# Graph network kernel: ranking counters laid out stream by stream, and row keys copied one step ahead

## The reference

```
edge_index = stack([src, dst])
h = relu(layernorm(x))
x = x + gcn(h, edge_index)      # sum over edges of h[src] * norm, by dst; layernorm, relu
h = relu(layernorm(x))
x = x + attention(h, edge_attr_128, edge_attr_128_n2, edge_index)
   # k, v: one row per edge; softmax and weighted sum over the edges of each src node, 4 heads
```

## Time and profile before

| | |
|---|---|
| median of 3 runs | 4865.36 us (4861.69 to 4885.93) |
| profiled execution | 4897.3 us, its span 4895.6 us |
| busy in the span | PE 69%, DVE 58%, ACT 50%, POOL 42% |
| POOL indirect scatters (L550) | 1612, 1894.3 us busy |
| ACT sums (L623) | 1616 activations, 883.3 us, and 308.6 us of accumulator reads |
| DVE products (L718) | 404, 380.1 us |
| DVE comparison with the ruler (L707) | 202, 196.5 us |

### The profile page before, as it was taken

How to read it: one execution, slowest core, us unless ns; L and a number is a source line. 1 busy time by engine, 2 the same in 40 slices (tenths; PEclk the granted TensorE clock), 3 DMA queues, 4 the chain that set the end, 5 groups by cost and what they waited for, 6 DMA issues and landing times. The chain is left out here.

```text
span 4895.6 us, 79918 instructions
## 1 busy us (share of the span) xinstructions
PE 3389.2 (69%) x21299; PEld 2441.0 (50%) x21299; DVE 2855.3 (58%) x5810; ACT 2454.4 (50%) x7415; POOL 2047.4 (42%) x1890
## 2 busy tenths in 40 slices
PE   3488767778777774021454567666668998999898
PEld 2266544455554452011333455555556776777665
DVE  6877787888887673530000455555556777777611
ACT  0545598888898784010232334333334665666411
POOL 1677287777777777777001433333331000000000
PEclk7655579999998897555555788888888999999855
DMA  1554144444444545456211566666666666666400
GB/s 59 168 173 163 49 138 162 155 160 160 161 151 157 170 160 183 142 170 208 88 33 53 187 207 222 216 208 214 212 209 196 189 190 203 189 189 190 132 0 26
DMA packets 511558, 764.21 MB, mean 156 GB/s; under 512 B 53848, under 2 KB 377408, under 8 KB 511358
## 3 DMA queue, kind: packets, MB, share of 16 engines
q1 hardware_dynamic: 406798, 522.56, 35.2%
q0 software_dynamic: 78160, 226.14, 12.2%
q10 hardware_dynamic: 26400, 13.21, 0.9%
HBM read 515.95 MB, written 245.75 MB: 156 GB/s over the span
## 5 line engine op out<-in xcount | busy, mean ns | idle before, releaser
L550 POOL DMA_INDIRECT table_s<-ring,place x1612 | 1894.3, 1175 | 1158.0 <-DMA ring<-in_kv 576.0
L623 ACT ACTIVATE row_base<-row_base 128x196 f32<-128x196 f32 x1616 | 883.3, 557 | 200.2 <-DVE row_base L718 189.5
L1346 PE MATMUL bank<-kT,G 128*128 128x384 f32 x1200 | 573.3, 562 | 235.9 <-ACT kT L1393 139.4
L1393 ACT COPY kT<-bank 128x384 f32<-128x384 f32 x600 | 286.5, 477 | 595.3 <-remote 264.6
L1366 PE MATMUL bank<-kv_rows,exT 128*128 128x129 f32 x3600 | 536.1, 288 | 0.0
L943 PE MATMUL bank<-xres 128*128 128x98 bf16 x3136 | 315.3, 236 | 291.4 <-ACT work L662 192.2
L1437 DVE TENSOR_REDUCE gmax<-bank 128x1 f32<-128x384 f32 x600 | 333.2, 555 | 299.2 <-remote 116.7
L962 PE MATMUL bank<-parts,work 128*128 128x384 bf16 x2401 | 501.2, 367 | 0.0
L1366 PEld LDWEIGHTS bank<-kv_rows,exT 128*128 128x128 f32 x3600 | 486.7, 205 | 0.1
L662 ACT CAST work<-bank 128x392 bf16<-128x392 f32 x784 | 373.1, 510 | 165.4 <-PE bank L943 98.3
L1017 DVE SCALAR_TENSOR_TENSOR others<-kv_rows,node_s,iota_h 128x384 bf16<-128x384 f32 x600 | 371.4, 619 | 135.1 <-DMA kv_rows<-table_s 79.2
(11 more groups left out here) (272 smaller groups left out, 4915.5 us busy)
## 6 DMA issues: line engine op xcount, KB each, us to landing
kv_rows<-table_s SPq DMA_DIRECT2D x600, 408.0 KB, 3.1
ring<-in_kv SPq DMA_DIRECT2D x402, 512.0 KB
G<-G_dram SPq DMA_DIRECT2D x600, 64.5 KB, 2.7
table_s<-ring,place POOLq DMA_INDIRECT x1612
G_dram<-gst ACTq DMA_DIRECT2D x50, 258.0 KB
x_dram<-xres SPq DMA_DIRECT2D x1, 3200.0 KB, 15.2
out<-ring SPq DMA_DIRECT2D x1, 3072.0 KB
table_s<-parts SPq DMA_DIRECT2D x6, 136.0 KB, 3.8
```

The costliest lines, as they stand in the source:

```text
L550: pool.indirect_dma_start(out=m["table_s"], out_offset=bass.IndirectOffsetOnAxis(ap=m["place"][0:n, i, k:k + 1], axis=0), in_=m["ring"][0: ...
L623: last = nc.scalar.activation(at, at, ACT.Identity, accum_out=m["place_f"][:, i % 2, h * STREAMS // 2 + k:h * STREAMS // 2 + k + 1])
L1346: pe.matmul(scores[k][:, 0:SGE], m["G"][:, u, 0:P], m["kT"][:, k, :], start=False, stop=True, skip_group_check=True).then_inc(m["scored"], 1)
```

## The change

**Layout.** A slot of the 1568 was tile * 8 + stream and is now stream * 196 + tile. The comparison, the four banks (two streams each now), the base rows, the products and what the sums read all follow. The ruler is stored once (196 elements) instead of eight times; in the comparison the ruler is now repeated over the streams, and the key is repeated along the 196 innermost elements. Before, the ruler was read as it lay, and eight keys side by side were repeated over the tiles. What ACT sums is now 196 elements side by side; they were four elements (16 bytes) apart.

**Halves.** The first half of the products now needs only the first two banks, so PE signals `ranked` twice per step, and `count` adds to two banks after each half of the products instead of to all four after both.

**Keys.** POOL copies the keys of step i + 1 before it issues the DMAs of step i (two copies in step 0). For that the rows of step i - 2 must have been sent, where it was i - 3.

**Shares.** `POOL_STEPS` goes from (132, 156) to (130, 152): two scatter steps leave the scatter block, the nodes block has 22 instead of 24, the last layer 50 instead of 46. The gathers' places are scaled with it: the first three stand behind POOL's step 27 instead of 28.

```
-POOL_STEPS = (132, 156)
+POOL_STEPS = (130, 152)
...
-        last = dve.tensor_copy(m["second_row"][one, :].rearrange("p (t s) -> p t s", s=STREAMS), m["second_base"][one, :, b * tiles:(b + 1) * tiles].rearrange("p s t -> p t s"))
+        last = dve.tensor_copy(m["second_row"][one, :], m["second_base"][one, :, :].rearrange("p s t -> p (s t)")[:, b * LANES_BANK:(b + 1) * LANES_BANK])
...
-            nc.scalar.copy(m["ruler"][:, :, :], column(m["iota_t"][:, :], [P, STILES, STREAMS])).then_inc(m["ruler_ready"], 1)
+            nc.scalar.copy(m["ruler"][:, :], m["iota_t"][:, :]).then_inc(m["ruler_ready"], 1)
...
 def scatter_rows(m, pool, i):
     u, first = i % KRING, STREAMS - columns(i)
-    need(pool, m["rows_sent"][u], sent_before(i))
-    pool.tensor_copy(m["ring"][:, u, first:STREAMS, KEY_AT:KEY_AT + 1], m["sources"][:, i, first:STREAMS].rearrange("p (s a) -> p s a", a=1)).then_inc(m["keys_ready"], 1)
+    for j in ((0, 1) if i == 0 else (i + 1,) if i + 1 < STEPS else ()):
+        v, at = j % KRING, STREAMS - columns(j)
+        need(pool, m["rows_sent"][v], sent_before(j))
+        pool.tensor_copy(m["ring"][:, v, at:STREAMS, KEY_AT:KEY_AT + 1], m["sources"][:, j, at:STREAMS].rearrange("p (s a) -> p s a", a=1)).then_inc(m["keys_ready"], 1)
     pool.wait_ge(m["places_ready"], i + 1)
     pool.wait_ge(m["rows_loaded"][u], 32 * (i // KRING + 1))
     pool.wait_ge(m["keys_ready"], i + 1)
...
-                        at = m["products"][:, h, :, k:k + 1].rearrange("p t a -> p (t a)")
+                        at = m["products"][:, h, k, :]
...
             def hot(i):
                 need(dve, m["counted"], i - 1)
-                dve.tensor_tensor(m["among"][:, i % 2, :].rearrange("p (t s) -> p t s", s=STREAMS), m["ruler"][:, :, :],
-                                  row_of(m["keys_t"][:, i, :], [P, STILES, STREAMS]), ALU.is_equal).then_inc(m["hot_ready"], 1)
+                dve.tensor_tensor(m["among"][:, i % 2, :].rearrange("p (s t) -> p s t", t=STILES), row_of(m["ruler"][:, :], [P, STREAMS, STILES]),
+                                  column(m["keys_t"][:, i, :], [P, STREAMS, STILES]), ALU.is_equal).then_inc(m["hot_ready"], 1)
...
-                dve.wait_ge(m["ranked"], i + 1)
                 for h in range(2):
-                    at = slice(h * STREAMS // 2, (h + 1) * STREAMS // 2)
+                    at = slice(h * RANK_BANKS // 2, (h + 1) * RANK_BANKS // 2)
+                    dve.wait_ge(m["ranked"], 2 * i + h + 1)
                     need(dve, m["half_summed"], 2 * i - 1 + h)
...
-                for b in range(RANK_BANKS):
-                    last = add(i, b, m["before_b"])
-                last.then_inc(m["ranked"], 1)
+                for h in range(2):
+                    for b in range(h * RANK_BANKS // 2, (h + 1) * RANK_BANKS // 2):
+                        last = add(i, b, m["before_b"])
+                    last.then_inc(m["ranked"], 1)
...
-                pe.wait_ge(m["selected"], 2 * i + 2)
-                for b in range(RANK_BANKS):
-                    last = add(i, b, m["not_before"])
+                for h in range(2):
+                    pe.wait_ge(m["selected"], 2 * i + h + 1)
+                    for b in range(h * RANK_BANKS // 2, (h + 1) * RANK_BANKS // 2):
+                        last = add(i, b, m["not_before"])
```

More of the change, by code:

```diff
@@ L966, in _ @@
             for b in range(RANK_BANKS):
-                pe.matmul(m["banks"][:, b, 0:LANES_BANK], m["ident"][:, :], base[:, b * tiles:(b + 1) * tiles, :], start=True, stop=True)
+                pe.matmul(m["banks"][:, b, 0:LANES_BANK], m["ident"][:, :], base[:, b * LANES_BANK:(b + 1) * LANES_BANK], start=True, stop=True)
             for i in range(STEPS):
```

14 lines of the change are left out of this document (5 added, 9 removed).

## The result

| | before | after |
|---|---|---|
| median of the runs | 4868.2 us (4 runs, 4861.7 to 4885.9) | 4948.3 us (4 runs, 4943.8 to 4989.9) |
| profiled execution: time / span | 4897.3 / 4895.6 us | 4943.8 / 4942.1 us |
| ratio of the times | | 1.0161, 95% interval 1.0117 to 1.0206 |

The changed kernel is slower, by 1.6%. The forecast was 4912 us with a range of 4840 to 4985.

The account below looks back on a forecast made before the run. GpSimd was taken to bound the scatter block, ending 95 us after the others. Scatter block +42, nodes block -25, last layer +32, front -2 make +47: 4944 us profiled, less 32 to the median, 4912; range 4840 to 4985.

Parts of the forecast that it names:

- start of the stretch: Scatter block, GpSimd's wait for the list of starts: longer comparisons on DVE delay it, +5 us, between 0 and 37.
- one step fewer: Scatter block: after the first gathers GpSimd does 102 steps instead of 103, -11 us.
- copy ahead: Scatter block: the 0.81 us gap behind each key copy loses 0.51 us over 102 steps, -52 us, or 0.
- holds on GpSimd: Scatter block: the longer comparison with two SBUF inputs holds GpSimd's scatters longer, +100 us, between 44 and 115.
- wait at the ring of keys: Scatter block: GpSimd's key copy waits for rows sent two steps before instead of three, said to cost nothing.
- nodes block: Nodes block: GpSimd is done 33 us sooner, so node tiles leave their slow pace earlier, -25 us.
- last layer: Last layer: four more GpSimd steps at 8.0 us each, +32 us.
- front: Front block: the second base row is read in order, its four copies take 3.3 us, -2 us.
- The comparison: Ranking on DVE: the key repeated along the innermost 196 lengthens it from 974 to 1786 ns, +0.81 us in 202 steps.
- the 0.77 of the prediction: Scatter block: measured holds, 258 us, against 337 estimated for freely falling scatters, since one hold often shields the next.
- the rival that the 0.81 us stay: Scatter and nodes blocks: the gap behind a key copy remains, so its savings don't come; +107, 4972 us, chance 0.18.
- The ranking as the bound: Scatter block: the ranking ends 163 us later, at 2075, passing GpSimd by 26; +73, 4938 us, chance 0.10.

Follow-up runs that it names:

- the layout alone: The changed kernel with the old key copy and POOL_STEPS back at (132, 156), halves included; 4534.9 us, 1.0148 of the kernel before, second kind of chip.
- The pairs: The changed kernel with each key stored twice side by side, so the comparison reads neighbouring pairs; 4382.5 us, 0.9807 of the kernel before, second kind.
- the copy ahead alone: The kernel before with only the row keys copied one step ahead, old layout and POOL_STEPS (132, 156); 4404.8 us against 4469.2, 0.9855, second kind.
- Pairs with the old shares: The changed kernel with each key stored twice and POOL_STEPS (132, 156); second kind 4355.7 us, 0.9746 of before; first kind 5112.2 us, 1.0516.
- eight that held nothing: The changed kernel with each step's comparison made as eight, one per stream, against a float32 scalar key; 4588.5 us, 1.0261 of before.

## Why the prediction was right

The direction and the range held, and the sum of +47 us met the difference of the profiled executions, 46.5. It did so by errors that cancel, so the closeness of the sum is luck:

| term | predicted | measured on the first kind |
|---|---|---|
| start of the stretch | +5 | 0, beside the front's -2 |
| one step fewer | -11 | -10 |
| copy ahead | -52 | -66; alone -64 on the second kind |
| holds on GpSimd | +100 | +71; the layout alone +66 on the second kind |
| wait at the ring of keys | 0 | +31.5 |
| passage to the next block | 0 | +6.6, on both kinds |
| nodes block | -25 | -7.7; on the second kind 22 or 24 steps make 0.3 us |
| last layer | +32 | +23.6; +12.6 on the second kind |
| front | -2 | -2 (first comparison at 121.3, not 123.5) |

- **The comparison**: 1784 ns, where 1786 were taken from L825. The pairs show that the repeated element is the reason.
- **The holds** are the largest mis-sized term, +71 where 100 were taken. That they exist, against the inference in the Trainium skill ("SBUF — State Buffer", "Who interferes with whom"), the scatter to 1865.42 above shows again, and the layout alone and the pairs show their price. The estimate from the length squared has the right proportion, if from two lengths only: a comparison's own holds went from 0.20 us (24.1 + 4.0 for copies, over 144) to 0.70 (89.5 + 12.1, over 146), where it had 0.28 and 1.03. But the 0.77 of the prediction stands for shielding at the old mix, and a longer comparison seems to shield more: from the copy ahead alone to after, the holds by the comparison of 2048 elements fell from 66.0 to 46.6 us. 71 is nearer to the lower end of the range given, 44 to 115, than to the 100 taken.
- **The copy ahead**: the mechanism was right, and the rival that the 0.81 us stay is out by the gap of 0.15 us. The size was not: the prediction let 0.30 us stand behind a copy as between two scatters, and 0.16 us is what stands there, so 66 us came and not 52. Its 11.3 us of waits for ACT's places were such gaps too.
- **The nodes block**: the step that failed is that GpSimd's earlier end is worth a fixed share of the tiles' pace. The slow stretch ended 25.5 us earlier, but two tiles fewer had passed in it.
- **The ranking as the bound**: the prediction gave it 0.10 and argued from DVE's free time. On the chip of the result it nearly came about (DVE's last work ends 4.8 us behind GpSimd's, and 4 us more would have made it the bound), through something else: stalls of about 196 us in front of the comparison where before had 85. Without them, on the second kind, DVE ends 96 us ahead of GpSimd even with the longer comparison; as a matter of DVE's time the rejection was right. What the stalls took in the profiled execution is the 31.5 us at the ring of keys, a term that the prediction didn't have. They are the largest difference between the kinds that the traces show (1.6% and 0.24% in the ratios); on the second kind the other terms nearly cancel.
- **The time**: 4912 was 36 us too low, since the distance of the profiled execution from the median was carried over from before. Between executions after varies by 46 us (4943.8 to 4989.9), which stalls that differ would explain; only one of them has a trace.
- **The narrower range** of the forecast, 4880 to 4930, doesn't follow from the bounds given for it: growth 88 to 115 and start 0 to 20 make 4895 to 4942.
- "GpSimd's last scatter about 90 us further from the last layer's start" came true: 1148.3 instead of 1064.4 us.

No version beat both kernels on both kinds of chip. Pairs with the old shares is the best on the second kind, by 2.5% over before and by 2.8% over after (0.9746 / 1.0024). On the first kind before remains best of those that ran there; the copy ahead alone wasn't tried on it.

## What to carry to other kernels

When a broadcast operand would repeat one element along the innermost run, store it twice and read pairs: the layout stays, and the comparison keeps its pace (971 ns instead of 1784). Where GpSimd's indirect DMAs bound a stretch, look at the length of each DVE instruction that reads two tiles in SBUF, not only at their sum; and measure every shorter form, since eight that held nothing made the others hold for longer. Measure such a kernel on more than one chip before it is called better: here a gain of 2.5% and a loss of 5.2% are the same program, and the slack of an engine that the trace shows as spare (95 us) can be what stalls use up.

## What the runs showed of the hardware

- A scatter that begins beside a DVE instruction with two SBUF operands ends 0.83 us after that instruction, or after the last of several in a row (one of 6.00 us through four). Beside the product with one operand in PSUM, and beside `tensor_scalar` with one tile operand, it takes its 0.96 us.
- Pairs of neighbouring bf16 elements are enough for the quick pace of the comparison: 1568 elements in 971 ns, 1784 with one element repeated.
- Behind a small GpSimd copy, an indirect DMA that needs it starts 0.81 us after its end, one that needs only an older copy after 0.15 us.
- ACT reads 196 float32 elements in 353 ns where they lie side by side and in 557 ns where neighbours are 16 bytes apart.
- Two kinds of chip: 210 to 221 or 279 to 289 GB/s at the most loaded, 4870 or 4470 us for the same kernel. On the first, DVE stands for up to 89 us at a time with no releaser in the trace, and PE and ACT with it for up to 64 and 59 us.
